# Gates, sums and layer norm between layers in one block, with the next weights' loads, and a last stage that stores by groups

## The chip, the cores and the metric

The kernel runs on 1 core of one Trainium2 chip. The metric is the device time of one execution in microseconds. The kernel before takes 5393.07 us, the median of 3 runs (5383.29 to 5398.34).

## The reference

The model has four layers on x of 16 sequences of 256 tokens of 128 features (4096 rows). Each layer normalises x, computes an attention branch s and a feed-forward branch g from the normalised rows, and adds their gated product:

```python
for layer in range(4):
    xn = _layernorm(x)              # (x - mean) / sqrt(var + 1e-5) over the 128 features
    s = attention[layer](xn)        # linear, gelu linear, causal softmax, small heads
    g = silu(feed_forward[layer](xn))   # local transformer, experts, routed, grouped
    x = x + s * g
return x
```

The last feed-forward is grouped: rows are cut into 8 groups of 512, and for each group h1 = x W1^T + b1 (128 to 512), h2 = h1 W2^T + b2 (512 to 128).

## The kernel before, in words

All rows stay in the core's memory: `core.x`, `core.xn` (normalised), `core.s` (attention branch), `core.y` (feed-forward branch) are each 128 partitions by 32 tiles by 128 features, `core.xnt` is the transpose of `xn` (features on partitions). One tile is 128 rows.

The program is a list of stages, one after the other (`stages`, lines 2969 to 2987). Each stage opens semaphores with `signals`, which clears them and puts a barrier of all engines; then comes a block, in which each engine has its own program and waits on semaphores; the block ends with a meeting of all engines, and `zero()` clears the semaphores again, with a barrier. So no engine starts on a stage before all engines have ended the one before.

For one layer the stages are these four.

- `layer_norm_stage` (line 297): VectorE takes the statistics of all 32 tiles (`bn_stats`, line 280), aggregates them (line 289), then computes 1/sqrt of the 32 variances in a chain of small operations, each waiting for the one before (lines 291 and 221 to 227), and writes the normalised rows, one scalar operation for each tile with mean and root as columns (line 293). TensorE transposes each tile (line 321), ScalarE copies four transposes at a time (line 329).
- the attention stage. Those of layers 0 and 1 begin by loading their weights with `load` (line 253), a block of its own that ends when all have landed; then comes the block that computes.
- the feed-forward stage. That of layer 0 uses the memory of `core.x` as room for other things, and so leaves in `core.x_in_memory` where the first x lies in DRAM.
- `combine_stage` (line 370): in four groups of 8 tiles ScalarE applies Silu to `core.y` (line 388), VectorE multiplies by `core.s` (line 394) and adds to `core.x` (line 398). In layer 0 SyncE issues the four loads of x there (line 383).

`grouped_ffn_stage` (from line 2834) is the last feed-forward. SyncE issues four loads for each of the 8 groups in its block (lines 2855 to 2858). TensorE turns W2 of group n (line 2867), multiplies W1 and b1 of group n - 1 by it (lines 2875 and 2878), and applies the merged matrix to the rows of group n - 2 (line 2888); ScalarE copies the turned W2 (line 2905), VectorE keeps the merged matrix and writes the group's 4 tiles to `core.y` (line 2920). After it `combine_stage` runs over all rows, and then one DMA stores all of x (line 2946).

`load(core, [x, ident])` at the start of the program (line 2938) loads all of x in one DMA, with the identity, in a block of its own.

Of the kernel before, what the change touches and what calls it, by code (L numbers as in the profile page):

```python
# [14 lines left out]
F32 = mybir.dt.float32  # L15
I32 = mybir.dt.int32
BF16 = mybir.dt.bfloat16
ALU = mybir.AluOpType
# [3 lines left out]
P = 128  # L22
# [124 lines left out]
def chain(eng, sem):  # L147

    n = [0]

    def after(ins):
        n[0] += 1
        ins.then_inc(sem, 1)
        eng.wait_ge(sem, n[0])

    return after
# [73 lines left out]
class Core:  # L230


    def __init__(self, nc, dram, ctx):
        self.nc, self.dram, self.stage, self.x_in_memory = nc, dram, 0, None
# [62 lines left out]
def layer_norm_stage(core):  # L297

    nc, bank, G = core.nc, core.bank, 4
    with ExitStack() as ctx:  # L300
        stats = ctx.enter_context(nc.sbuf_tensor(core.name("ln_stats"), [P, NT, 6], F32))
        mv = ctx.enter_context(nc.sbuf_tensor(core.name("ln_mv"), [P, NT, 2], F32))
        rstd = ctx.enter_context(nc.sbuf_tensor(core.name("ln_rstd"), [P, NT], F32))
        tmp = ctx.enter_context(nc.sbuf_tensor(core.name("ln_tmp"), [P, NT], F32))
        (dve_step, rows_ready, turned, copied), zero = ctx.enter_context(
            signals(nc, [core.name(n) for n in ("ln_dve_step", "ln_rows_ready", "ln_turned", "ln_copied")]))
        with nc.Block() as block:
            @block.vector
            def _(dve):
                after = chain(dve, dve_step)  # L310
                tiles = [core.x[:, j, :] for j in range(NT)]
                for ins in normalise_rows(nc, after, tiles, [core.xn[:, j, :] for j in range(NT)], stats, mv, rstd, tmp, 1e-5):
                    ins.then_inc(rows_ready, 1)

            @block.tensor
            def _(pe):
                for j in range(NT):
                    pe.wait_ge(rows_ready, j + 1)
                    if j % G == 0 and j >= 2 * G:
                        pe.wait_ge(copied, j // G - 1)  # L320
                    ins = nc.tensor.transpose(bank[j // G % 2][:, (j % G) * P:(j % G + 1) * P], core.xn[:, j, :], core.ident[:, :])
                    if j % G == G - 1:
                        ins.then_inc(turned, 1)

            @block.scalar
            def _(act):
                for g in range(NT // G):
                    act.wait_ge(turned, g + 1)
                    nc.scalar.copy(core.xnt[:, g * G * P:(g + 1) * G * P], bank[g % 2][:, :]).then_inc(copied, 1)
        zero()  # L330
# [39 lines left out]
def combine_stage(core):  # L370

    nc, G = core.nc, 8
    reload, core.x_in_memory = core.x_in_memory, None
    with ExitStack() as ctx:
        (gated, multiplied, added), zero = ctx.enter_context(signals(nc, [core.name(n) for n in ("cb_gated", "cb_multiplied", "cb_added")]))
        x_in, zero_in = ctx.enter_context(signals(nc, [core.name(f"cb_x_in{i}") for i in range(NT // G)]))
        groups = [slice(i * G, (i + 1) * G) for i in range(NT // G)]
        with nc.Block() as block:
            @block.sync
            def _(sp):  # L380
                if reload is not None:
                    for i, g in enumerate(groups):
                        sp.dma_start(core.x[:, g, :], reload[:, g, :]).then_inc(x_in[i], 16)

            @block.scalar
            def _(act):
                for g in groups:
# [2602 lines left out]
```

## Time and profile before

| what | value |
|---|---|
| median of 3 runs | 5393.07 us |
| profiled execution | 5392.81 us, of which 5391.0 us are the span of the trace |
| busy, share of the span | TensorE 88%, weight loads 62%, VectorE 69%, ScalarE 52%, GpSimd 52% |
| mean granted TensorE clock | 0.934 |

Busy time is an average over stages that are very unlike each other: the feed-forward stage of layer 0 alone (in which TensorE is nearly always busy) fills the first 3570 us or so. The stages run one after the other, so a passage between two stages is to be read by itself, in the timeline.

### The profile page before, as it was taken

To read this page: it belongs to the slowest core of one execution; us is meant where nothing else is said; L and a number is where in the kernel's file an instruction comes from. 1 tells how busy PE (TensorE), PEld (TensorE's weight loads), DVE (VectorE), ACT (ScalarE), POOL (GpSimd) and SP (SyncE) were. 2 spreads that over 40 slices of the span, in tenths; PEclk is the share of its full clock that TensorE was granted. 3 is DMA by queue.
4 is the path that set the end of the run, shared out by engine and by line. 5 is a ranking of instruction groups with operands and counts; after the bars stand their busy time and mean duration, and the time that the engine had idled before them with its cause. 6 is when DMAs were issued, how large, how long until landed. Compare 5 with 4: busy or idle time off the path is not lost. (4 is left out here: it accounts for less than half of the span.)

```text
span 5391.0 us, 143191 instructions
## 1 busy us (share of the span) xinstructions
PE 4720.6 (88%) x57069; PEld 3338.6 (62%) x57103; DVE 3708.4 (69%) x8589; ACT 2807.9 (52%) x6208; POOL 2810.1 (52%) x3349
## 2 busy tenths in 40 slices
PE   7699999999999999999999999955375999845886
PEld 3367676666667767666676667744363667623665
DVE  7677777777777777777777777746725656577443
ACT  2266666666666666666666666621023666641342
POOL 4477776777677767776777777701122333311000
PEclk9799999999999999999999999977587999967898
DMA  0211111111111111111111110000211000010012
GB/s 21 66 35 25 25 35 37 25 25 33 32 29 25 35 31 29 25 35 33 29 25 34 22 28 21 18 24 2 77 52 24 2 2 2 1 25 13 26 29 58
DMA packets 312165, 150.62 MB, mean 28 GB/s; under 512 B 146143, under 2 KB 301004, under 8 KB 311244
## 3 DMA queue, kind: packets, MB, share of 16 engines
q1 hardware_dynamic: 309451, 137.20, 10.5%
q8 instruction: 461, 7.55, 0.6%
q0 software_dynamic: 2048, 4.20, 0.3%
q14 instruction: 205, 1.67, 0.1%
HBM read 101.10 MB, written 27.41 MB: 24 GB/s over the span
## 5 line engine op out<-in xcount | busy, mean ns | idle before, releaser
L1450 POOL TENSOR_TENSOR loc_a<-loc_a,loc_b 128x512 f32<-128x512 f32 x768 | 977.2, 1272 | 598.3 <-DVE loc_b L1526 598.3
L1127 PE MATMUL psum<-loc_wqk,loc_xt 128*128 128x512 f32 x1536 | 837.6, 628 | 12.3 <-DVE loc_b L1526 5.9
L1195 PE MATMUL psum<-loc_m,xn_rows 128*128 128x128 f32 x6144 | 843.7, 280 | 3.8 <-DVE y_rows L1558 2.6
L1475 POOL TENSOR_TENSOR loc_a<-loc_a,loc_rn 128x512 f32<-128x512 f32 x768 | 784.9, 1043 | 0.1
L1195 PEld LDWEIGHTS psum<-loc_m,xn_rows 128*128 128x128 f32 x6144 | 745.6, 192 | 55.9 <-issue 36.0
L1319 ACT ACTIVATE loc_sq<-psum 128x512 f32<-128x512 f32 x768 | 456.1, 594 | 449.6 <-PE psum L1127 443.2
L1522 DVE TENSOR_TENSOR loc_a<-psum,loc_rope 128x512 f32<-128x512 f32 x768 | 523.9, 682 | 174.9 <-ACT loc_sq L1319 161.7
L1356 ACT COPY xn_rows<-psum 128x512 f32<-128x512 f32 x768 | 412.3, 589 | 326.6 <-PE psum L1183 324.3
L1482 POOL TENSOR_TENSOR xn_cols<-xn_cols,loc_rec 128x512 f32<-128x512 f32 x384 | 392.3, 1042 | 307.5 <-DVE loc_rec L1553 307.5
L1135 PEld LDWEIGHTS psum<-ident,loc_a 128*128 128x128 f32 x3072 | 347.7, 142 | 317.9 <-issue 307.1
L1526 DVE TENSOR_TENSOR loc_b<-psum,loc_rope 128x512 f32<-128x512 f32 x768 | 520.8, 678 | 0.0
L1530 DVE TENSOR_REDUCE loc_n<-loc_sq 128x8 f32<-128x512 f32 x768 | 517.1, 673 | 0.0
L1135 PE MATMUL psum<-ident,loc_a 128*128 128x128 f32 x3072 | 477.0, 278 | 10.4 <-ACT loc_qt L1337 7.2
L769 POOL TENSOR_TENSOR l2a_p<-l2a_p,l2a_rec 128x256 f32<-128x256 f32 (+1 forms) x256 | 211.5, 826 | 441.5 <-DVE l2a_rec L756 441.5
L1183 PE MATMUL psum<-xn_cols,loc_x 64*128 64x256 f32 x3072 | 435.6, 402 | 1.1 <-ACT xn_rows L1356 0.9
L1537 DVE TENSOR_REDUCE loc_top<-psum 128x8 f32<-128x512 f32 x384 | 247.3, 686 | 236.7 <-PE psum L1158 236.7
L1337 ACT COPY loc_kt<-psum 128x512 f32<-128x512 f32 x384 | 224.7, 585 | 306.2 <-PE psum L1135 306.2
L1158 PE MATMUL psum<-loc_kt,loc_qt 64*32 64x64 f32 x24576 | 333.8, 223 | 3.2 <-issue 2.5
L1158 PEld LDWEIGHTS psum<-loc_kt,loc_qt 64*32 64x32 f32 x24576 | 295.0, 105 | 50.8 <-issue 39.6
L1168 PEld LDWEIGHTS psum<-ident,xn_cols 128*128 128x128 f32 x1536 | 181.2, 141 | 225.1 <-issue 225.1
L1127 PEld LDWEIGHTS psum<-loc_wqk,loc_xt 128*128 128x128 f32 x1536 | 232.7, 191 | 122.2 <-issue 59.7
L1183 PEld LDWEIGHTS psum<-xn_cols,loc_x 64*128 64x128 f32 x3072 | 264.4, 186 | 67.2 <-issue 10.4
(370 smaller groups left out, 8532.2 us busy)
## 6 DMA issues: line engine op xcount, KB each, us to landing
loc_x<-loc_shifted SPq DMA_DIRECT2D x192, 256.0 KB, 4.0
loc_shifted<-y_rows SPq DMA_DIRECT2D x144, 64.0 KB
loc_wqk<-in_L_ffn_Wqkv SPq DMA_DIRECT2D x24, 256.0 KB, 3.8
x_rows<-y_rows SPq DMA_DIRECT2D x96, 64.0 KB
x_rows<-y_rows SPq DMA_DIRECT2D x96, 63.5 KB
moe_w<-in_L_ffn_W SPq DMA_DIRECT2D x16, 256.0 KB, 5.0
l3a_qk<-l3a_rot SPq DMA_DIRECT2D x16, 256.0 KB, 2.1
grp_w<-in_L_ffn_W SPq DMA_DIRECT2D x16, 256.0 KB, 4.2
```

The costliest lines, as they stand in the source:

```text
L1127: nc.tensor.matmul(ring("p", i, unit), xt[:, b % 2, t * P:(t + 1) * P], wqk[:, unit * 512:(unit + 1) * 512], start=True, stop=True).then_i ...
L1135: last = nc.tensor.transpose(turn_bank[:, j * P:(j + 1) * P], a[:, (UNITS * i + unit) % (3 * UNITS), j * P:(j + 1) * P], core.ident[:, :])
L1158: last = nc.tensor.matmul(score_bank[h][32 * w:32 * w + 32, 64 * j:64 * j + 64], qt[rows_h, i % 2, j, 32 * w:32 * w + 32], kt[rows_h, b % ...
L1183: last = nc.tensor.matmul(u_bank[h][:, 256 * v:256 * v + 256], x2[rows_h, b % 3, WPT * t + w, :], pt[rows_h, i % 2, :, 32 * w:32 * w + 32] ...
L1195: last = nc.tensor.matmul(y_bank[:, 0:P], u[:, i % 2, h // 2, h % 2, :], m[:, h, :], start=(h == 0), stop=(h == HEADS - 1))
L1319: nc.scalar.activation(sq[:, g % 2, :], ring("p", i, unit), ACT.Square).then_inc(sem["squared"], 1)
L1356: nc.scalar.copy(to, u_bank[h].rearrange("p (w j q) -> p w j q", w=2, j=PAIRS)).then_inc(sem["u_copied"], 1)
L1450: nc.gpsimd.tensor_tensor(part, part, b_[:, g % 2, :], ALU.add).then_inc(sem["added"], 1)
L1475: nc.gpsimd.tensor_tensor(part, part, rn[:, i % 2, 8 * unit:8 * unit + 8].rearrange("p (h e) -> p h e", e=1).to_broadcast([P, 8, DH]), ALU ...
L1522: nc.vector.tensor_tensor(a[:, g % (3 * UNITS), :].rearrange("p (h d) -> p h d", d=DH), src.rearrange("p (h d) -> p h d", d=DH), cos, ALU. ...
L1526: nc.vector.tensor_tensor(b_[:, g % 2, :].rearrange("p (h s d) -> p h s d", s=2, d=32), halves, sin, ALU.mult).then_inc(sem["rotated"], 1)
L1530: nc.vector.tensor_reduce(n2[:, i % 2, 8 * unit:8 * unit + 8], sq[:, g % 2, :].rearrange("p (h d) -> p h d", d=DH), AX.X, ALU.add).then_in ...
```

## The change

- `combine_stage` of a layer and `layer_norm_stage` of the next are one block, `enter_layer_stage`. Silu stays with ScalarE in four groups of 8 tiles. The products go to GpSimd. VectorE adds group by group and takes the statistics of each group right after its sum. Aggregation and the chain of the root are done for each half of the tiles (16 each): for the first half after two groups, for the second at the end. GpSimd normalises the 16 tiles of the first half, VectorE those of the second. TensorE and ScalarE transpose and copy as before.
- The weights of the attention of layers 0 and 1, and of the grouped feed-forward (biases of all 8 groups, matrices of the first four), are loaded by SyncE in that block; it waits for them at its end. The loading blocks of those stages go. The other attention stages keep their loads.
- At the start of the program x comes in four DMAs by the same block (layer 0, without gates, products and sums), and the identity and the weights behind it.
- `grouped_ffn_stage` loads the matrices of groups 4 to 7 itself, applies Silu (ScalarE), product (GpSimd) and sum (VectorE) to each group of 4 tiles after its store, and stores each group of x to DRAM in a DMA of its own. The last `combine_stage` and the single store go.

```diff
-def combine_stage(core):
-def layer_norm_stage(core):
...
+def enter_layer_stage(core, weights=None):
+    nc, bank, layer = core.nc, core.bank, core.layer
+    core.layer += 1
+    G, T, HALF = 8, 4, NT // 2
+    arriving, core.x_in_memory = core.x_in_memory, None
+    core.weights = weights(core) if weights else None
+    loads = core.weights.loads if weights else []
...
+            @block.sync
+            def _(sp):
+                if arriving is not None:
+                    for i, g in enumerate(groups):
+                        sp.dma_start(core.x[:, g, :], arriving[:, g, :]).then_inc(sem[f"x_in{i}"], 16)
+                if layer == 0:
+                    sp.dma_start(core.ident[:, :], core.dram["ident"]).then_inc(sem["ident_in"], 16)
+                for dst, src in loads:
+                    sp.dma_start(dst, src).then_inc(sem["loaded"], 16)
+                if loads:
+                    sp.wait_ge(sem["loaded"], 16 * len(loads))
+
+            @block.vector
+            def _(dve):
+                after = chain(dve, sem["dve_step"])
+
+                def gather(i, g):
+                    if arriving is not None:
+                        dve.wait_ge(sem[f"x_in{i}"], 16)
+                    if layer > 0:
+                        dve.wait_ge(sem["multiplied"], i + 1)
+                        nc.vector.tensor_tensor(core.x[:, g, :], core.y[:, g, :], core.x[:, g, :], ALU.add).then_inc(sem["added"], 1)
+                        dve.wait_ge(sem["added"], i + 1)
+                    for j in range(g.start, g.stop):
+                        last = nc.vector.bn_stats(stats[:, j, :], core.x[:, j, :])
+                    return last
+
+                def measure(h):
+                    for j in range(h.start, h.stop):
+                        last = nc.vector.bn_aggr(mv[:, j, :], stats[:, j, :])
+                    after(last)
+                    after(nc.vector.tensor_scalar(mv[:, h, 1], mv[:, h, 1], 1e-5, None, ALU.add))
+                    rsqrt(nc, after, rstd[:, h], mv[:, h, 1], tmp[:, h])
+
+                for n, h in enumerate(halves):
+                    for i in (2 * n, 2 * n + 1):
+                        last = gather(i, groups[i])
+                    after(last)
+                    measure(h)
+                    scales.append(after.count[0])
+                for j in range(HALF, NT):
+                    nc.vector.tensor_scalar(core.xn[:, j, :], core.x[:, j, :], mv[:, j, 0:1], rstd[:, j:j + 1], ALU.subtract,
+                                            ALU.mult).then_inc(sem["dve_rows"], 1)
+
+            @block.gpsimd
+            def _(pool):
+                if layer > 0:
+                    for i, g in enumerate(groups):
+                        pool.wait_ge(sem["gated"], i + 1)
+                        nc.gpsimd.tensor_tensor(core.y[:, g, :], core.y[:, g, :], core.s[:, g, :], ALU.mult).then_inc(sem["multiplied"], 1)
+                pool.wait_ge(sem["dve_step"], scales[0])
+                for j in range(HALF):
+                    nc.gpsimd.tensor_scalar(core.xn[:, j, :], core.x[:, j, :], mv[:, j, 0:1], rstd[:, j:j + 1], ALU.subtract,
+                                            ALU.mult).then_inc(sem["pool_rows"], 1)
...
 def grouped_ffn_stage(core):
...
             @block.sync
             def _(sp):
+                for g in range(NG // 2, NG):
+                    for dst, src in own.matrices(core, g, w1[g], w2[g]):
+                        sp.dma_start(dst, src).then_inc(late[g - NG // 2], 16)
                 for g in range(NG):
-                    sp.dma_start(w2[:, g, :, :], dram["L3_ffn_W2"][g, :, :].rearrange("p (c o) -> p c o", o=P)).then_inc(loaded[g], 16)
...
+                    sp.wait_ge(sem["added"], g + 1)
+                    sp.dma_start(core.out[:, rows(g), :], core.x[:, rows(g), :]).then_inc(sem["sent"], 16)
+                sp.wait_ge(sem["sent"], 16 * NG)
...
             @block.scalar
...
+                for n in range(NG + 3):
+                    if n < NG:
+                        keep_turned(n)
+                    if 0 <= n - 3 < NG:
+                        gate(n - 3)
...
             @block.vector
...
-                for n in range(NG + 2):
+                for n in range(NG + 4):
                     if 0 <= n - 1 < NG:
                         keep_merged(n - 1)
                     if 0 <= n - 2 < NG:
                         store(n - 2)
+                    if 0 <= n - 4 < NG:
+                        add(n - 4)
...
 def stages():
     return [
+        lambda core: enter_layer_stage(core, LinearWeights), linear_attention_stage, local_transformer_stage,
+        lambda core: enter_layer_stage(core, GeluWeights), gelu_linear_attention_stage, experts_stage,
+        enter_layer_stage, causal_attention_stage, routed_ffn_stage,
+        lambda core: enter_layer_stage(core, GroupedWeights), small_head_attention_stage, grouped_ffn_stage,
     ]
```

## Rows read from the trace of the kernel before

**Rows 1.** Page, part 1: busy us of each engine, share of the span, instructions.

```profile
PE 4720.6 (88%) x57069; PEld 3338.6 (62%) x57103; DVE 3708.4 (69%) x8589; ACT 2807.9 (52%) x6208; POOL 2810.1 (52%) x3349
```

**Rows 2.** Timeline, layer 0 to 1: start, duration in us, engine, line, idle before, releaser.

```profile
3573.03 1.28 ACT L388 ACT_TABLE_LOAD   x1 [7.21 <-PEq L141]
3573.05 4.06 SPq L383 DMA_DIRECT2D x_rows<-in_L_attn_x  x4
3575.42 1.23 DVE L394 TENSOR_TENSOR y_rows<-y_rows,s_rows 128x1024 f32<-128x1024 f32 x1 [6.03 <-ACT y_rows L388]
3577.50 1.23 DVE L398 TENSOR_TENSOR x_rows<-y_rows,x_rows 128x1024 f32<-128x1024 f32 x1 [0.85 <-DMA x_rows<-in_L_attn_x]
...
3587.50 6.28 DVE L280 BATCH_NORM_STATS2 ln_stats<-x_rows 128x6 f32<-128x128 f32 x32 [1.60 <-PEq L141]
3593.82 2.22 DVE L289 BATCH_NORM_AGGREGATE ln_mv<-ln_stats 128x2 f32<-128x6 f32 x32
...
3598.97 8.29 DVE L293 TENSOR_SCALAR xn_rows<-x_rows,ln_mv,ln_rstd 128x128 f32<-128x128 f32 x32
...
3607.69 0.58 ACT L329 COPY xn_cols<-psum 128x512 f32<-128x512 f32 x1 [0.44 <-PE psum L321]
...
3619.54 0.87 PE L1663 MATMUL psum<-ident,l1a_w 128*128 128x128 f32 x3 [11.89 <-PEq L141]
```

**Rows 3.** Timeline, layer 1 to 2.

```profile
4064.13 1.28 ACT L388 ACT_TABLE_LOAD   x1 [33.68 <-PEq L141]
...
4097.79 0.58 ACT L329 COPY xn_cols<-psum 128x512 f32<-128x512 f32 x1 [0.44 <-PE psum L321]
```

**Rows 4.** Timeline, the start of the program.

```profile
1.54 0.91 SPq L261 DMA_DIRECT2D x_rows<-in_L_attn_x  x1
...
13.18 6.28 DVE L280 BATCH_NORM_STATS2 ln_stats<-x_rows 128x6 f32<-128x128 f32 x32 [13.18 <-PEq L141]
...
33.37 0.58 ACT L329 COPY xn_cols<-psum 128x512 f32<-128x512 f32 x1 [0.44 <-PE psum L321]
...
43.43 1.65 PE L435 MATMUL psum<-l0a_w,xn_cols 128*128 128x384 f32 x2 [10.11 <-DVE l0a_ones L549]
```

**Rows 5.** Timeline, the last feed-forward stage.

```profile
5330.65 0.37 SPq L2855 DMA_DIRECT2D grp_w<-in_L_ffn_W  x1
...
5337.77 1.11 PE L2867 MATMUL psum<-ident,grp_w 128*128 128x128 f32 x4 [9.95 <-DMA grp_b<-in_L_ffn_b]
...
5339.81 1.11 PE L2867 MATMUL psum<-ident,grp_w 128*128 128x128 f32 x4 [0.92 <-DMA grp_b<-in_L_ffn_b]
...
5365.99 0.69 DVE L2920 TENSOR_TENSOR y_rows<-psum,grp_offset 128x512 f32<-128x512 f32 x1 [0.20 <-PE psum L2888]
```

**Rows 6.** GpSimd's groups by shape: busy us, mean ns of one, idle before.

```profile
L1450 POOL TENSOR_TENSOR loc_a<-loc_a,loc_b 128x512 f32<-128x512 f32 x768 | 977.2, 1272 | 598.3 <-DVE loc_b L1526 598.3
...
L364 POOL TENSOR_TENSOR s_rows<-s_rows,l1a_gamma 128x1024 f32<-128x1024 f32 x2 | 4.9, 2447 | 16.3 <-DVE s_rows L293 16.3
...
L2373 POOL TENSOR_SCALAR cd_w1h<-cd_w1h,cd_gh 128x512 f32<-128x512 f32 x1 | 1.6, 1633 | 0.0
L2372 POOL TENSOR_SCALAR cd_w1l<-cd_w1l,cd_gl 128x64 f32<-128x64 f32 x1 | 0.5, 477 | 0.0
```

**Rows 7.** Timeline, VectorE's operations while GpSimd works and while it doesn't.

```profile
4765.32 8.27 POOL L2369 TENSOR_TENSOR y_rows<-xn_rows,cd_rn 128x512 f32<-128x512 f32 x8
...
4770.57 0.98 DVE L2436 SCALAR_TENSOR_TENSOR cd_base<-cd_base,cd_top 16x1 f32<-16x1 f32 x1
...
4773.66 0.14 DVE L2436 SCALAR_TENSOR_TENSOR cd_base<-cd_base,cd_top 16x1 f32<-16x1 f32 x1
...
3712.63 16.80 DVE L293 TENSOR_SCALAR s_rows<-s_rows,bn_mv,bn_rstd 128x128 f32<-128x128 f32 x32
```

**Rows 8.** Page, part 6: DMAs of 256 KB, us from issue to landing.

```profile
l3a_qk<-l3a_rot SPq DMA_DIRECT2D x16, 256.0 KB, 2.1
grp_w<-in_L_ffn_W SPq DMA_DIRECT2D x16, 256.0 KB, 4.2
```

More of the change, by code:

```diff
@@ L325, in _ @@
             @block.scalar
             def _(act):
-                for g in range(NT // G):
-                    act.wait_ge(turned, g + 1)
-                    nc.scalar.copy(core.xnt[:, g * G * P:(g + 1) * G * P], bank[g % 2][:, :]).then_inc(copied, 1)
+                if layer > 0:
+                    for g in groups:
+                        nc.scalar.activation(core.y[:, g, :], core.y[:, g, :], ACT.Silu).then_inc(sem["gated"], 1)
+                for q in range(NT // T):
+                    act.wait_ge(sem["turned"], q + 1)
+                    nc.scalar.copy(core.xnt[:, q * T * P:(q + 1) * T * P], bank[q % 2][:, :]).then_inc(sem["copied"], 1)
@@ L367, in layer_norm_of_branch @@
         zero()
-def combine_stage(core):
[L372 to L387, printed above, removed]
-                    nc.scalar.activation(core.y[:, g, :], core.y[:, g, :], ACT.Silu).then_inc(gated, 1)
-            @block.vector
-            def _(dve):
-                for i, g in enumerate(groups):
-                    dve.wait_ge(gated, i + 1)
-                    nc.vector.tensor_tensor(core.y[:, g, :], core.y[:, g, :], core.s[:, g, :], ALU.mult).then_inc(multiplied, 1)
-                    dve.wait_ge(multiplied, i + 1)
-                    if reload is not None:
-                        dve.wait_ge(x_in[i], 16)
-                    nc.vector.tensor_tensor(core.x[:, g, :], core.y[:, g, :], core.x[:, g, :], ALU.add).then_inc(added, 1)
-        zero()
-        zero_in()
 def linear_attention_stage(core):
@@ L559, in linear_attention_stage @@
         zero()
+    own.ctx.close()
 class Softmax:
@@ L1802, in gelu_linear_attention_stage @@
         layer_norm_of_branch(core, 1e-12, gamma[:, :], beta[:, :])
+    own.ctx.close()
 def experts_stage(core):
@@ L2905, in _, with gate @@
                     nc.scalar.copy(w2t[:, g % 2, :, :], turn_bank[g % 2].rearrange("p (c q) -> p c q", c=CH)).then_inc(sem["w_ready"], 1)
+                def gate(g):
+                    act.wait_ge(sem["stored"], g + 1)
+                    nc.scalar.activation(core.y[:, rows(g), :], core.y[:, rows(g), :], ACT.Silu).then_inc(sem["gated"], 1)
+                for n in range(NG + 3):
[3 more added lines that the diff above has]
+                        gate(n - 3)
+            @block.gpsimd
+            def _(pool):
+                for g in range(NG):
+                    pool.wait_ge(sem["gated"], g + 1)
+                    nc.gpsimd.tensor_tensor(core.y[:, rows(g), :], core.y[:, rows(g), :], core.s[:, rows(g), :], ALU.mult).then_inc(sem["multiplied"], 1)
             @block.vector
```

164 lines of the change are left out of this document (89 added, 75 removed).

## The prediction

> **What bounds the kernel now.** I read first the page's busy times: TensorE is busy 4720.6 us, 88% [rows 1], but nearly all of that lies inside the long stages, which the change leaves alone. Then I read the timeline at the four places where one layer hands over to the next, and at the end. There nearly every engine idles while one works. Between layers 0 and 1 [rows 2]: from the table load for the Silu (3573.03) to the end of the last copy (3607.69 + 0.58 = 3608.27) are 35.24 us, and VectorE works in 30 of them: products and sums (3575.42 to 3585.90, where the wait of 1.60 begins), statistics (6.28), aggregation (2.22), the root's chain of 13 small operations (3593.82 + 2.22 = 3596.04 to 3598.97, 2.93 us) and 32 rows of 0.26 us (8.29). Then nothing runs for 11.27 us until the weights, whose loads start only now, let TensorE begin (3619.54). The place after layer 1 is the same without the wait for x (0.85 in rows 2): 34.24 us [rows 3]; the one after layer 2 is its like, so there are two of these, and their next stages load for themselves, which doesn't change. At the start [rows 4], VectorE waits for all of x until 13.18, the last copy ends at 33.95, the first product of the attention is at 43.43: 9.48 us of loading. At the end [rows 5], TensorE waits for the first weights from 5330.65 to 5337.77, the last group is stored at 5366.68, and the remaining 24.3 us are Silu, products, sums and one store of all of x one after the other.
>
> **Barriers.** Between the last sum and the statistics VectorE waits 1.60 us [rows 2]; three clearings with their barriers and the block's ends lie there, so one barrier is about 0.5 us, and 1.5 us is what stays of a passage without loads.
>
> **Start of the program.** x comes in quarters. The reload's first quarter, issued at 3573.05, let the sum start at 3577.50 [rows 2], some 4.3 us later; from 1.54 [rows 4] that is 5.9. Eight statistics are 6.28 / 4 = 1.6. The second quarter is in at about 7.8 (2 MB had landed by about 11.5, as VectorE starts at 13.18 after barriers); its statistics end at 9.4, 16 aggregations 1.1 and the chain 2.9 give 13.4. From there GpSimd normalises the first 16 tiles.
>
> **The price of a GpSimd row** is the term that decides, and no row has it: a 128x128 scalar operation with two scalars of a column each. With one such scalar 128x64 took 477 ns and 128x512 took 1633 [rows 6]; on the line between them 128 elements are 0.64 us. The lower bound is the line of the two-input operations, 2447 ns at 1024 and 1272 at 512 [rows 6], so 0.39 at 128; the upper is twice 0.64 = 1.28, if the second operation is a second pass. I take 0.75 (0.64 and a little for the second scalar), with its handover 0.8. VectorE's price for the same row is 0.26 [rows 2].
>
> **Who blocks whom.** GpSimd ran eight operations in a row from 4765.32, 8.27 us [rows 7]. Inside it VectorE's operation on one element with two inputs took 0.98 us, right behind it, without GpSimd, 0.14. And 32 rows of the kind that take 8.29 us alone took 16.80 us from 3712.63, with GpSimd's products over part of it. So VectorE's sums, two-input chain operations and rows wait for the end of the GpSimd operation in progress; GpSimd waits as long for them. The statistics read one tensor and I cost them free. During a row of GpSimd operations VectorE then gets one such operation through for each.
> The Trainium skill (SBUF — State Buffer, Who interferes with whom) has this as a rule: GpSimd and VectorE share one port pair, taken for a whole instruction, and VectorE needs it in two-port modes or with two inputs from SBUF against a GpSimd operation that reads. By that rule the new block's parallel work is largely serial again, and the sum is the one below; without it the sum would be the first rival's.
>
> Start, continued: VectorE does the other statistics (3.1, to 16.6) and aggregation (17.7), four chain operations on one input (0.9, 18.6), nine on two inputs at 0.8 each (25.8). GpSimd ends at 13.4 + 16 x 0.8 = 26.3. The 16 rows left take 4.15 (30.4), transposing and copying the last group 1.0 as in rows 2 (3607.26 to 3608.27): 31.3, against 33.95: **-2.6**. The nine weights are issued behind x and land long before. So the 9.48 us of loading become a passage of 1.5: **-8.0**. Together -10.6.
>
> **Between the layers**, clock from the table load. Silu of group 0 is done at 2.4 (3573.03 to 3575.42). GpSimd multiplies 2.45 us a group [rows 6] where VectorE took 1.2: 2.4 to 4.85, and goes straight on with group 1 (to 7.3), so the first sum waits for that. Sum 1.2 (8.5), product 2 (to 10.95) beside the statistics, sum 1 (12.15), product 3 (14.6) beside statistics (13.8) and aggregation (14.9), chain 2.9: 17.8. Now GpSimd's 16 rows of 0.8 plus the two sums that hold it up for 1.2 each: 17.8 + 12.8 + 2.4 = 33.0. VectorE: sum 2 waits one row (18.6 to 19.8), statistics (21.4), sum 3 (21.8 to 23.0), statistics (24.6), aggregation (25.7), four chain operations (26.6), eight at 0.8 until GpSimd is through, one more (33.2), 16 rows (37.4), tail 1.0: 38.4. Before: 34.2. One barrier pair of the old combining block goes (0.5). So **+3.7** each after layers 1 and 2; after layer 0 38.4 - 35.24 - 0.5 = +2.7 (x is in at 4.4, before the first product is), and the 11.27 of loading become 1.5: **-7.1** in all.
> Cover of the loads: SP's queue. Layer 3's 24 loads (eight matrices, sixteen vectors) are the most; before, eight loads of these kinds were in 9.16 us after the first issue (5330.65 to 5339.81, rows 5), so 24 at that pace are 27.5 us, under 38. If they weren't, the block's end would wait for them. In layer 1 eleven loads queue behind x's four quarters, nothing that VectorE waits for stands behind them.
>
> **The last stage.** The block starts as before at about 5330.6, but groups 0 to 3 are there: 7.1 us off, and 0.9 for the wait of group 1 [rows 5]. Groups 4 to 7 are issued at once and land about 4.2 us after issue [rows 8], needed over 12 us later. TensorE's cadence stays, as the added Silu and sum stand behind the copies and stores that TensorE waits for, on engines with slack. Tail from the last store at 5366.68 (old clock): Silu of half a width 0.6; GpSimd is then still at group 6's product (1.27 us, to 67.7), group 7's to 69.0, sums of 0.7 for 6 and 7 to 70.4. The 256 KB store: 2.1 to 4.2 us for that size [rows 8], I take 3.1; two clearings that the old end didn't have 1.0, close 0.4: 75.0. Against 5391.0 that is -16.0, and with the 8.1 at the start **-24.1**.
>
> **Sum.** -10.6 - 7.1 + 2 x 3.7 - 24.1 = -34.4 us. The profiled execution took 5392.8 (span 5391.0 and 1.8 around it), the median of the runs is 5393.1: 5358.4, so 5358.
>
> **Bounds.** With a row at 0.39 on GpSimd (0.45 with handover): GpSimd ends at 27.4, the chain at 29.0, rows and tail 34.2, so -0.5 twice, -11.3 after layer 0, -15.0 at the start: -51 in all, 5341. With 1.28 (1.33): 17.8 + 21.3 + 2.4 = 41.5, end 46.2, so +11.5 twice, +0.7, -2.8 at the start: -3, 5390. That is about 60 us per us of a row.
>
> **Rivals.**
> A, nothing blocks: on other shapes or forms of operands the two engines may run beside each other, as VectorE's statistics do. Then the chain ends at 14.5, GpSimd's rows at 26.5, TensorE's 16 last transposes (0.26 each) and a copy at 31.3: -3.4 twice, -14.2, -11.6 at the start, -24.1: 5335. For it: GpSimd's own times hardly vary. Against it: rows 7.
> B, GpSimd's rows become the bound at 1.05 to 1.6 us: the gain of loads and end is given back in three blocks, within 16 us (0.3%, what this measurement can tell from none): about 5385. For it: its scalar form is dearer per element (1633 at 512) than the two-input one (1272).
> C, slower: the same place at 2.0 us a row, beyond twice the one-scalar price. Each us costs 64 here (16 rows, four blocks), so from the -3 at 1.28: +43, 5436; it is slower than can be overlooked from 1.6 us on. Against it: no row of that kind.
> D, the prefetch doesn't help, because the loads outlast their block: for layer 3 they would have to take over 38 us, 1.6 each; it would cost a few us only: within the range.
>
> **Chances.** Forecast (row 0.55 to 1.05, blocking): 0.60, own range 5346 to 5377. A, or a still cheaper row: 0.22. B: 0.12. C: 0.05; D 0.01. Faster 0.83, same 0.12, slower 0.05. Range: 5334 to 5384, from A's time into B's.
>
> **What would show it.** In the new block: GpSimd's row between 0.6 and 0.9 us; a sum of VectorE of 2 to 3.5 us instead of 1.22, or started late, while a product runs; chain operations of 0.8 instead of 0.19 in the second half; VectorE's rows ending 37 us after the table load. Passages without loads of 1.5 us; first transposes of the last stage 2.5 us after the previous copy; the last store issued 4 us after the last group. Wrong: sums of 1.22 us beside products (A), rows over 1 us (B, C), or a block that ends on SP's wait (D).

## The result and the profile after

The changed kernel takes 5344.54 us, the median of 4 runs (5338.56 to 5351.56), beside 5392.26 us before (4 runs, 5383.29 to 5398.34): ratio 0.9913, 95% interval 0.9894 to 0.9932. Measured again on another chip it took 5342.65 us (5 runs) beside 5389.07 (9 runs), ratio 0.9913 (0.9895 to 0.9931). Forecast were 5358, range 5334 to 5384: the time lies in the range, but 1.5 us below the 5346 to 5377 that the prediction gave its own case, and the gain is 47.7 us where 34.4 were forecast.

The profiled execution took 5351.56 us, the slowest of its four, with a span of 5349.7, against 5392.8 and 5391.0. The page's busy times move little (TensorE's by +23 us), but for GpSimd's, which grow by 103 us beside [rows 1]:

```profile
span 5349.7 us, 142952 instructions
PE 4743.6 (89%) x57103; PEld 3342.8 (62%) x57103; DVE 3698.6 (69%) x8565; ACT 2811.1 (53%) x6212; POOL 2913.3 (54%) x3433
```

So the gain is in the passages, and they must be read one by one. The start of the program, from the timeline (start, duration, engine, line, operation, idle before, releaser), beside [rows 4]:

```profile
5.63 1.64 DVE L404 BATCH_NORM_STATS2 en_stats<-x_rows 128x6 f32<-128x128 f32 x8 [5.63 <-DMA x_rows<-in_L_attn_x]
...
13.11 12.73 POOL L432 TENSOR_SCALAR xn_rows<-x_rows,en_mv,en_rstd 128x128 f32<-128x128 f32 x16 [12.66 <-DVE en_rstd L228]
...
21.21 4.46 DVE L421 TENSOR_SCALAR xn_rows<-x_rows,en_mv,en_rstd 128x128 f32<-128x128 f32 x16
...
25.89 4.18 PE L446 MATMUL psum<-ident,xn_rows 128*128 128x128 f32 x17 [0.34 <-POOL xn_rows L432]
...
30.11 0.59 ACT L457 COPY xn_cols<-psum 128x512 f32<-128x512 f32 x1 [0.41 <-PE psum L446]
...
32.05 1.65 PE L527 MATMUL psum<-l0w_w,xn_cols 128*128 128x384 f32 x2 [1.99 <-DVE l0a_ones L641]
```

The first product comes at 32.05 instead of 43.43. GpSimd's 16 rows take 12.73 us, 0.80 each. All 64 of its rows, by their tile (shortest, median and longest in ns, first and last start in us):

```profile
L432 POOL TENSOR_SCALAR xn_rows<-x_rows,en_mv,en_rstd x64: 783/797/1828, 13.1 to 4912.3; 128x128 f32<-128x128 f32 x64
```

The block between layers 1 and 2, beside [rows 3] (that between layers 0 and 1 [rows 2] is like it, 36.25 us long):

```profile
4038.13 1.28 ACT L454 ACT_TABLE_LOAD   x1 [33.64 <-PEq L141]
...
4040.56 11.23 POOL L429 TENSOR_TENSOR y_rows<-y_rows,s_rows 128x1024 f32<-128x1024 f32 x4 [10.30 <-ACT y_rows L454]
4042.95 3.35 DVE L401 TENSOR_TENSOR x_rows<-y_rows,x_rows 128x1024 f32<-128x1024 f32 x1 [10.27 <-POOL y_rows L429]
...
4055.22 1.23 DVE L401 TENSOR_TENSOR x_rows<-y_rows,x_rows 128x1024 f32<-128x1024 f32 x1
4055.30 14.24 POOL L432 TENSOR_SCALAR xn_rows<-x_rows,en_mv,en_rstd 128x128 f32<-128x128 f32 x16 [3.50 <-DVE en_rstd L228]
...
4062.53 0.32 DVE L222 TENSOR_SCALAR en_tmp<-en_mv 128x16 int32<-128x16 int32 x1
...
4064.45 0.17 DVE L226 TENSOR_TENSOR en_tmp<-en_rstd 128x16 f32<-128x16 f32 x1
4064.65 0.17 DVE L227 TENSOR_TENSOR en_tmp<-en_tmp,en_mv 128x16 f32<-128x16 f32 x1
...
4064.86 0.33 DVE L228 SCALAR_TENSOR_TENSOR en_rstd<-en_tmp,en_rstd 128x16 f32<-128x16 f32 x1
...
4066.00 4.54 DVE L421 TENSOR_SCALAR xn_rows<-x_rows,en_mv,en_rstd 128x128 f32<-128x128 f32 x16
...
4069.59 3.90 PE L446 MATMUL psum<-ident,xn_rows 128*128 128x128 f32 x17 [0.35 <-POOL xn_rows L432]
...
4072.81 1.30 ACT L457 COPY xn_cols<-psum 128x512 f32<-128x512 f32 x2 [0.27 <-PE psum L446]
```

The first sum takes 3.35 us where it takes 1.22 alone: it waits until GpSimd's second product is through. VectorE's rows are done at 4070.54, only a microsecond behind GpSimd's (4069.54). What ends the block is TensorE: it transposes the tiles in order, waits until 4069.5 for GpSimd's last, and makes that one and VectorE's 16 in a row from there (x17). ScalarE's copies of them end at 4074.11, 35.98 us after the table load.

The end, beside [rows 5]:

```profile
5310.67 0.37 ACT L2838 COPY s_rows<-psum 128x256 f32<-128x256 f32 x1 [0.80 <-PE psum L2775]
...
5313.45 1.94 PE L2961 MATMUL psum<-ident,l3w_w 128*128 128x128 f32 x8 [2.82 <-PEq L141]
...
5341.05 0.68 DVE L3035 TENSOR_TENSOR x_rows<-y_rows,x_rows 128x512 f32<-128x512 f32 x1
...
5341.65 0.68 DVE L3030 TENSOR_TENSOR y_rows<-psum,grp_offset 128x512 f32<-128x512 f32 x1
...
5342.25 3.71 DVE L3035 TENSOR_TENSOR x_rows<-y_rows,x_rows 128x512 f32<-128x512 f32 x3
```

TensorE starts 2.4 us after the previous stage's last copy instead of 9.5; the last group is written at 5342.33, and 7.4 us later all is over, where 24.3 followed before.

By places (microseconds; a second profile of the same kernel in the fourth column):

| place | before | after | after, again | forecast of the difference |
| --- | --- | --- | --- | --- |
| start to first product | 43.43 | 32.05 | 32.0 | -10.6 |
| table load to TensorE, layer 0 to 1 | 46.51 | 37.61 | 37.7 | -7.1 |
| the same, layer 1 to 2 | 48.3 | 50.2 | 50.6 | +3.7 |
| the same, layer 2 to 3 | 43.9 | 44.7 | 44.8 | +3.7 |
| last copy of the small heads to the end | 62.8 | 38.7 | 38.9 | -24.1 |
| sum of these | 244.9 | 203.3 | 204.0 | -34.4 |
| small-head attention, layer 3 | 377.4 | 384.6 | 373.9 | 0 |
| all the rest | 4768.7 | 4761.8 | 4762.9 | 0 |

### The profile page after: what moved, and what is told of

Read it like the earlier page. It is cut to its first block and busy times, and to the rows that moved or that the text cites. A ratio compares the mean times of both kernels' runs of the same rounds, so it can differ in the third digit from the quotient of the medians.

```text
span 5349.7 us, 142952 instructions
## 1 busy us (share of the span) xinstructions
PE 4743.6 (89%) x57103; PEld 3342.8 (62%) x57103; DVE 3698.6 (69%) x8565; ACT 2811.1 (53%) x6212; POOL 2913.3 (54%) x3433
## 5 line engine op out<-in xcount | busy, mean ns | idle before, releaser
L1288 PEld LDWEIGHTS psum<-loc_m,xn_rows 128*128 128x128 f32 x6144 | 744.9, 191 | 55.6 <-issue 35.4
L1276 PEld LDWEIGHTS psum<-xn_cols,loc_x 64*128 64x128 f32 x3072 | 264.4, 186 | 67.3 <-issue 10.7
```

The costliest lines, as they stand in the source:

```text
L1276: last = nc.tensor.matmul(u_bank[h][:, 256 * v:256 * v + 256], x2[rows_h, b % 3, WPT * t + w, :], pt[rows_h, i % 2, :, 32 * w:32 * w + 32] ...
L1288: last = nc.tensor.matmul(y_bank[:, 0:P], u[:, i % 2, h // 2, h % 2, :], m[:, h, :], start=(h == 0), stop=(h == HEADS - 1))
```

## The experiments

All start from the changed kernel. The first four were timed beside the kernel before at 5389.02 us (13 runs).

**Products on VectorE.**

```diff
...
                     if layer > 0:
+                        dve.wait_ge(sem["gated"], i + 1)
+                        nc.vector.tensor_tensor(core.y[:, g, :], core.y[:, g, :], core.s[:, g, :], ALU.mult).then_inc(sem["multiplied"], 1)
                         dve.wait_ge(sem["multiplied"], i + 1)
...
-                        nc.gpsimd.tensor_tensor(core.y[:, g, :], core.y[:, g, :], core.s[:, g, :], ALU.mult).then_inc(sem["multiplied"], 1)
```

> The products of the three blocks between layers go back from GpSimd to VectorE, nothing else changes. Theory (the sums wait for GpSimd's products, which take 2.45 us and hold the sums up, 3.3 and 1.7 us instead of 1.22): VectorE does product 1.2, sum 1.2 and statistics 1.65 of a group without waits, the first half's chain ends at 2.4 + 2 x 4.05 + 3.9 = 14.4 us after the table load instead of 17.1, GpSimd's rows at 27.2, the last copy at about 32 instead of 36.0: 4 us less in each of three blocks, -12 in all. Rival (GpSimd takes 4.9 us of products off VectorE, and the waits are only slack): the block gets longer by up to 4.9, +10 to +15 in all.

Measured: 5334.52 us (5328.81 to 5336.26), ratio 0.9898 (0.9881 to 0.9914). The blocks are 36.5, 34.5 and 35.0 us long instead of 36.3, 36.0 and 35.8: some 2 us in all, neither the gain nor the loss that was expected. The start of the rows shows where it went: they begin at 14.65 us instead of 17.17, but take longer:

```profile
4053.55 15.46 POOL L430 TENSOR_SCALAR xn_rows<-x_rows,en_mv,en_rstd 128x128 f32<-128x128 f32 x16 [22.47 <-DVE en_rstd L228]
```

15.46 us instead of 14.24, as two products more of VectorE stand in their way. What VectorE gains ahead of the rows it gives back in part beside them. After layer 0 it gains less ahead of them, as its first product comes only when x's first quarter is there, 4.2 us after the table load (3558.40) instead of 2.4:

```profile
3562.61 1.23 DVE L401 TENSOR_TENSOR y_rows<-y_rows,s_rows 128x1024 f32<-128x1024 f32 x1 [7.49 <-DMA x_rows<-in_L_attn_x]
```

The rest of the difference between the two profiles is the small-head stage, 368.3 us in this one (below).

**All rows on VectorE.**

```diff
-                for j in range(HALF, NT):
-                    nc.vector.tensor_scalar(core.xn[:, j, :], ...).then_inc(sem["dve_rows"], 1)
+                    for j in range(h.start, h.stop):
+                        nc.vector.tensor_scalar(core.xn[:, j, :], ...).then_inc(sem["dve_rows"], 1)
...
-                for j in range(HALF):
-                    nc.gpsimd.tensor_scalar(core.xn[:, j, :], ...).then_inc(sem["pool_rows"], 1)
```

> GpSimd normalises no rows: VectorE writes the 16 of each half right after that half's root. Products stay on GpSimd. Theory (16 rows are 12.7 to 14.2 us on GpSimd and 4.15 on VectorE, and the block ends when GpSimd's rows and then 16 transposes are through): between layers VectorE is through at 17.1 + 4.2 + 2 x 2.85 + 3.9 + 4.2 = 35.1, last copy 36.0, as now; at the start 13.0 + 4.2 + 3.2 + 3.9 + 4.2 = 28.5, last copy 29.4 instead of 30.7. In all -1, no difference that can be told. Rival (GpSimd's rows are a gain, as they run beside VectorE): +4.2 in each of four blocks, +17.

Measured: 5339.94 us (5338.00 to 5340.71), ratio 0.9909 (0.9892 to 0.9926). The blocks take 36.19, 36.20 and 36.19 us, within 0.4 of the changed kernel's; at the start the last copy ends at 29.7 instead of 30.7. GpSimd's 51 us of rows in four blocks buy nothing. Why: the same place, between layers 1 and 2:

```profile
4070.14 4.19 DVE L420 TENSOR_SCALAR xn_rows<-x_rows,en_mv,en_rstd 128x128 f32<-128x128 f32 x16
4070.55 4.32 PE L438 MATMUL psum<-ident,xn_rows 128*128 128x128 f32 x16 [9.44 <-DVE xn_rows L420]
```

Here VectorE's second half is the last work and transposes run beside it. In the changed kernel that work is done sooner, but the transposes come after it.

**Loads back where they were.** The loading blocks stand at the head of the attention stages of layers 0 and 1 again, and the last stage issues all its loads itself.

```diff
-    loads = core.weights.loads if weights else []
+    loads = []
...
+        load(core, own.loads)
...
-                for g in range(NG // 2, NG):
+                for g in range(NG):
```

> No weights are loaded in the blocks between layers: the attention of layers 0 and 1 load in a block of their own as before, the grouped feed-forward loads all in its own block. Theory (the loads are fully hidden in the new kernel): +8.0 at the start, +9.8 after layer 0, +7.1 in the last stage, +25 in all; the blocks between layers keep their lengths (30.7 and 36). The small-head attention took 384.6 us in the profile of the changed kernel against 377.5 before. If the weights that lie in memory during it or their loads are the cause, it is back at 377; if it is a variation between executions, it falls anywhere between, whatever is loaded. Rival (part of the prefetch is paid in the blocks): less than +20.

Measured: 5370.43 us (10 runs, 5356.22 to 5381.30), ratio 0.9959 (0.9948 to 0.9971), 26 more than the changed kernel. Places: first product at 40.2 (+8.2), between layers 0 and 1 46.9 us from table load to TensorE (+9.3), first product of the last stage 9.0 us after the copy (+6.6), together 24.1; the eight groups of the last stage take 0.8 us more besides (29.6 instead of 28.9), which makes the 25 expected:

```profile
3607.49 0.59 ACT L457 COPY xn_cols<-psum 128x512 f32<-128x512 f32 x1 [0.41 <-PE psum L446]
3609.68 0.34 SPq L263 DMA_DIRECT2D l1w_w<-in_L_attn_Wq  x1
...
3618.67 0.88 PE L1752 MATMUL psum<-ident,l1w_w 128*128 128x128 f32 x3 [11.22 <-PEq L141]
```

The blocks keep their length (36.35, 36.37 and 35.61 us; the first and the last of them have the loads beside them in the changed kernel, 36.25 and 35.79), so the loads cost nothing where they stand now. The small-head stage took 377.5 us, as in the kernel before. Alone that would fit its rival, that the weights in memory slow it; but it took 377.5 in the kernel with products of half a width too, which has the loads ahead, and the last two experiments take this up.

**The old end.** Its edit takes the stores, gates, products and sums out of the last block and runs the old stages behind it:

```diff
-                for g in range(NG):
-                    sp.wait_ge(sem["added"], g + 1)
-                    sp.dma_start(core.out[:, rows(g), :], core.x[:, rows(g), :]).then_inc(sem["sent"], 16)
...
+def combine_stage(core):
+    ...
+def store_stage(core):
+    ...
```

> The last stage only writes its branch, then come the old combining block over all rows and the single store; the weights of groups 0 to 3 are still loaded ahead. Theory (tail of 24.3 us from the last store of the branch to the end before, 7.4 now, and a cadence of 3.11 us a group that is TensorE's either way): +17. Rival (the added Silu, product, sum and DMA of each group slow the groups): the 8 groups become shorter than the present 28.9 us from first transpose to last store of the branch, and the difference is below +15.

Measured: 5368.56 us (5359.51 to 5375.46), ratio 0.9957 (0.9940 to 0.9973). From the last group's write to the end 24.91 us instead of 7.37, that is +17.5; the groups before it take 28.6 us against 28.9, so what was added between them costs 0.3 us (where, see the last stage below). The medians' 24 are more than that; the small-head stage, 388.0 us here, varies by as much.

**Products of half a width.** To see whether a sum waits for the GpSimd operation in progress or for the whole run of them.

```diff
-                        dve.wait_ge(sem["multiplied"], i + 1)
+                        dve.wait_ge(sem["multiplied"], 2 * (i + 1))
...
-                        nc.gpsimd.tensor_tensor(core.y[:, g, :], core.y[:, g, :], core.s[:, g, :], ALU.mult).then_inc(sem["multiplied"], 1)
+                        for part in (slice(g.start, g.start + 4), slice(g.start + 4, g.stop)):
+                            nc.gpsimd.tensor_tensor(core.y[:, part, :], core.y[:, part, :], core.s[:, part, :],
+                                                    ALU.mult).then_inc(sem["multiplied"], 1)
```

> GpSimd multiplies each group of 8 tiles in two operations of 4 tiles (1.2 to 1.3 us each) instead of one of 2.45. Theory (a sum of VectorE waits for the end of the GpSimd operation in progress, then runs at its own speed): the first sum of a block takes 1.2 + 1.2 = 2.4 us instead of 3.35. Rival (the two engines share the memory's bandwidth as long as both run): it stays near 3.3, as GpSimd's products fill the same time. The block's length changes by less than 1 us either way.

```profile
4041.21 11.79 POOL L430 TENSOR_TENSOR y_rows<-y_rows,s_rows 128x512 f32<-128x512 f32 x8 [10.30 <-ACT y_rows L456]
4043.73 2.27 DVE L401 TENSOR_TENSOR x_rows<-y_rows,x_rows 128x1024 f32<-128x1024 f32 x1 [10.41 <-POOL y_rows L430]
```

The first sum takes 2.27 us instead of 3.35: 1.1 us less, about half a product. So it waits for the operation in progress. One run took 5345.06 us; the blocks 35.98, 35.82 and 35.57.

**GpSimd's rows as operations on two inputs.** The same 16 rows, each as two operations that read x and the root's column. This kernel leaves out the mean of these tiles and serves for its times alone.

```diff
-                    nc.gpsimd.tensor_scalar(core.xn[:, j, :], core.x[:, j, :], mv[:, j, 0:1], rstd[:, j:j + 1], ALU.subtract,
-                                            ALU.mult).then_inc(sem["pool_rows"], 1)
+                    for part in (spare[:, j, :], core.xn[:, j, :]):
+                        ins = nc.gpsimd.tensor_tensor(part, core.x[:, j, :], rstd[:, j:j + 1].to_broadcast([P, P]), ALU.mult)
+                    ins.then_inc(sem["pool_rows"], 1)
```

> GpSimd writes each of its 16 rows with two operations of two inputs (x by the root, spread over the row; the first into a spare tile), about 0.35 us each, instead of one scalar operation of 0.8: it is busy about as long, with another kind of operation. Left out: the mean is not subtracted in these 16 tiles. Open is why VectorE's root chain took only 3.68 us (17.46 to 21.14 at the start of the program) beside GpSimd's scalar rows, where I had 8.1. Theory (a scalar operation on GpSimd reaches into memory only part of its time, an operation with two inputs nearly all of it): beside these rows VectorE's nine chain operations on two inputs take 0.3 to 0.5 us instead of 0.17 to 0.33, the chain 4.5 us or more, and its 16 rows in part too over 4.5 us. Rival (operations of 16 elements are too short to be held up much by anything): chain of 3.7 us or less as now.

```profile
4049.37 1.22 DVE L402 TENSOR_TENSOR x_rows<-y_rows,x_rows 128x1024 f32<-128x1024 f32 x1
4049.41 1.44 POOL L434 TENSOR_TENSOR en_spare<-x_rows,en_rstd 128x128 f32<-128x128 f32 x1 [3.48 <-DVE en_rstd L228]
...
4058.72 0.33 DVE L226 TENSOR_TENSOR en_tmp<-en_rstd 128x16 f32<-128x16 f32 x1
4058.97 0.39 POOL L434 TENSOR_TENSOR xn_rows<-x_rows,en_rstd 128x128 f32<-128x128 f32 x1
4059.08 0.32 DVE L227 TENSOR_TENSOR en_tmp<-en_tmp,en_mv 128x16 f32<-128x16 f32 x1
4059.33 0.39 POOL L434 TENSOR_TENSOR en_spare<-x_rows,en_rstd 128x128 f32<-128x128 f32 x1
```

Beside these every operation of the chain takes 0.32 us and they follow each other by 0.36, the distance of GpSimd's own: one passes for each of GpSimd's, as the prediction had it for all GpSimd work. Both ways: a GpSimd operation of 0.39 us that meets a sum takes 1.44. The 13 operations of the chain take 4.5 us, against 3.6 beside the scalar rows (4056.31 to 4060.83 here). One run took 5326.02 us; its blocks are 35.5, 35.5 and 35.4, and its small-head stage 368.1.

**The first half's rows on ScalarE**, with the products on VectorE, and then with the products on GpSimd. The core of both:

```diff
-                    nc.gpsimd.tensor_scalar(core.xn[:, j, :], ...)
...
+                        if j < HALF:
+                            nc.scalar.activation(core.xn[:, j, :], core.x[:, j, :], ACT.Identity, bias=minus[:, j:j + 1],
+                                                 scale=rstd[:, j:j + 1]).then_inc(sem["pool_rows"], 1)
```

`minus`, the mean times the root with its sign turned, is one more operation of VectorE.

> Products on VectorE, and ScalarE, which is idle after the Silu, writes the first half's 16 rows (root as scale, one more small operation on VectorE for the bias -mean x root); GpSimd does nothing in the block. Theory (what ends the block is GpSimd's 16 rows and the 16 transposes behind them; without them it is VectorE's own work): first half's chain at 14.6, VectorE's second half 8.1 + 3.9 to 26.7, 16 rows to 30.9, last copy at 31.8 after the table load instead of 36.0, at the start 26 instead of 30.7: -4.2 in three blocks and -4.7, -17 in all against the changed kernel. Rival (VectorE and the handovers bound the block either way): blocks of 34 to 35 as with the products alone, -5 in all.

> As the changed kernel, products on GpSimd, but the first half's 16 rows on ScalarE. Theory: first half's chain at 17.3 (the sums of the first half still wait for products, 2.7 us), then VectorE without neighbours: two sums and statistics 5.7, 3.9, 4.2, so 31.1 and last copy at 32.0; at the start 26 as with e7. -4 in three blocks and -4.7 against the changed kernel, -17: taking the products away from GpSimd brings nothing beyond. Rival (the products are the costlier part): blocks of 34 to 35.

Measured beside the kernel before at 5393.32 us (7 runs): 5327.00 us (5323.48 to 5333.28), ratio 0.9870 (0.9854 to 0.9887), with the products on VectorE; 5332.78 us (5326.86 to 5341.11), ratio 0.9888 (0.9872 to 0.9905), on GpSimd. The blocks: 34.2, 32.3, 32.2 and 32.2, 32.3, 32.2; the last copy of the start ends at 25.6 in both, where 30.7 was. In the first kernel VectorE's first product after layer 0 waits for x's reload, as above, hence 34.2. But for that block both theories hold (31.8 and 32.0 expected), and the rivals' 34 to 35 falls: once GpSimd has no rows, it makes no difference to the later blocks which of the two engines multiplies. The second kernel:

```profile
4049.71 3.19 ACT L459 ACTIVATE xn_rows<-x_rows,en_minus,en_rstd 128x128 f32<-128x128 f32 x8 [12.10 <-DVE en_minus L421]
4050.26 3.17 PE L446 MATMUL psum<-ident,xn_rows 128*128 128x128 f32 x8 [44.16 <-ACT xn_rows L459]
...
4059.39 4.19 DVE L425 TENSOR_SCALAR xn_rows<-x_rows,en_mv,en_rstd 128x128 f32<-128x128 f32 x16
4059.79 4.32 PE L446 MATMUL psum<-ident,xn_rows 128*128 128x128 f32 x16 [2.32 <-DVE xn_rows L425]
```

ScalarE's rows follow each other by 0.40 us, half of GpSimd's 0.80, and hinder VectorE in nothing that is seen: 16 rows 4.19, as where VectorE writes all of them, and the first half is transposed long before the second comes. VectorE's rows end 31.2 us after the table load, against 32.4 in the changed kernel. So of the 3.7 us by which this block is shorter, 1.3 are VectorE's earlier end, and 2.4 are the transposes that no longer stand behind GpSimd's rows.

**The changed kernel and the last one again**, on one chip.

> The changed kernel once more, nothing edited. Theory: the small-head stage of layer 3 takes between 368 and 388 us in one execution and another whatever the program (377.4 in the kernel before, 384.6 in the changed one, 368.1 to 388.0 in the experiments), while the blocks between the layers repeat within 0.4 us. So this profile shows blocks of 36.2 +- 0.4 us (from table load to the end of the last copy) after each layer, a start of 32.0, a tail of 7.4, and a small-head stage that differs from 384.6 by several us, with the span moved by the same; the median is 5344 +- 6. Rival: 384.6 us is a property of the changed kernel (its loads or its placement in memory slow that stage): then the stage is within 2 us of 384.6 again.

> The kernel of the experiment in which ScalarE normalises the first sixteen tiles, once more and beside the changed kernel on the same chip. Theory: its three blocks are 3.8 us shorter each and its start 5 us shorter, 16.4 in all, so the difference of the medians is 16 us once the varying stage is averaged over more runs (11.7 were measured with four runs of each). Rival: it is less than 8 us, because TensorE's stages behind the shorter blocks take back what the blocks gain.

Measured beside 5389.07 us (9 runs): 5342.65 us (5339.29 to 5351.89), and 5328.78 us (5326.84 to 5332.61), ratio 0.9887 (0.9867 to 0.9906). The small-head stage in four profiles, as stretches (from, to, length; busy us of TensorE, its weight loads, VectorE, ScalarE, GpSimd; granted clock; DMA share; GB/s): after, after again, the kernel with two-input rows, the old end.

```profile
4926.40:5311.00 384.60, 332.80 (x5312) 237.18 (x5312) 157.36 (x304) 136.16 (x289) 20.35 (x16) 0.87 0.08 24
```

```profile
4928.00:5301.90 373.90, 327.21 (x5312) 233.16 (x5312) 157.50 (x304) 136.04 (x289) 20.33 (x16) 0.88 0.08 25
```

```profile
4917.40:5285.50 368.10, 320.39 (x5312) 229.66 (x5312) 157.45 (x304) 135.88 (x289) 20.29 (x16) 0.90 0.08 26
```

```profile
4929.90:5317.90 388.00, 337.23 (x5312) 240.88 (x5312) 157.52 (x304) 136.43 (x289) 20.34 (x16) 0.86 0.08 24
```

The same number of instructions, the same kernel even in the first two, and 10.7 us apart; in these four, the longer the stage, the lower its granted clock (0.86 to 0.90) and the longer TensorE is busy. The rival, that 384.6 belongs to the changed kernel, falls. Where two profiles have this stage alike, 373.9 and 373.8, their spans are 5340.8 and 5324.7: ScalarE's rows are worth 16.1 us, where 16.4 were expected and the blocks and starts of these two profiles give 16.9; the medians say 13.9, and the rival's less than 8 falls. Which of the two kernels with ScalarE's rows is faster is not shown: the medians were 5327.00 with the products on VectorE and 5332.78 on GpSimd, with ranges that overlap, while the blocks of the second are 2 us shorter in all.

## Why the prediction held, and where not

The time fell into the stated range, and the loads, the price of a row and the last stage came as reckoned; what happens inside the blocks between layers did not.

**Start, forecast -10.6, came -11.4.** GpSimd's rows began at 13.1 (13.4 forecast), took 0.80 each with handover (0.80) and ended at 25.8 (26.3). Passage to the first product 1.4 us (1.5). The mechanism at the end was another: not VectorE's rows, but the transposes behind GpSimd's.

**The price of a row**, which decided, was right: 0.797 us in the median, inside the bounds of 0.39 and 1.28, and the value taken was 0.75.

**A sum beside products**: forecast 3.7 for the wait and the sum (4.85 to 8.5), came 3.35. The half-width products show that the wait ends with the operation in progress. The chain of the first half ends at 17.1 (17.8 forecast). The third sum was to wait for a row of GpSimd; it was issued first instead, took 1.23 us, and GpSimd's first row took the 1.83 above.

**The step that failed: "eight at 0.8 until GpSimd is through".** It took the 0.98 us of one operation beside GpSimd's two-input products [rows 7] for the price of every two-input operation beside any GpSimd work. Beside the scalar rows the chain of 13 operations took 3.6 us between the layers (25.7 to 33.2, 7.5 us, forecast) and 3.7 at the start (8.1 forecast); undisturbed it is 2.7. Only one in three of the nine on two inputs waits, for 0.15 us, and three of them pass in 0.78 us, the time of one row. In the changed kernel the one that waits is always line 228's; it is the moment that counts and not the form, for in the kernel with the loads back it is line 226's at the start of the program:

```profile
20.15 0.32 DVE L226 TENSOR_TENSOR en_tmp<-en_rstd 128x16 f32<-128x16 f32 x1
```

The two-input rows of the experiment bring back one operation for each of GpSimd's. Two things that were costed free of any hold weren't: of the four chain operations on one input three took 0.32 to 0.39 us instead of 0.17 (all four 1.35 us, 0.9 forecast), and VectorE's 16 rows take 4.5 us beside GpSimd's, where 4.15 were forecast.

The trace of the kernel before could have told this. The prediction reads the 0.14 us of 4773.66 [rows 7] as an operation without GpSimd beside it. But GpSimd was at work then, on one of the very scalar operations of [rows 6], and the same operation took 0.14 inside the next one too:

```profile
4773.58 0.48 POOL L2372 TENSOR_SCALAR cd_w1l<-cd_w1l,cd_gl 128x64 f32<-128x64 f32 x1
4773.66 0.14 DVE L2436 SCALAR_TENSOR_TENSOR cd_base<-cd_base,cd_top 16x1 f32<-16x1 f32 x1
...
4774.05 1.63 POOL L2373 TENSOR_SCALAR cd_w1h<-cd_w1h,cd_gh 128x512 f32<-128x512 f32 x1
...
4775.08 0.14 DVE L2436 SCALAR_TENSOR_TENSOR cd_base<-cd_base,cd_top 16x1 f32<-16x1 f32 x1
```

So the 0.98 and the 0.14 differ by the form of GpSimd's operation, and not by whether GpSimd works.

The Trainium skill (SBUF — State Buffer, Who interferes with whom) says that whoever issues first has the shared pair for its whole instruction. For GpSimd's two-input operations the runs agree (3.35 and 2.27 us for the sum, 0.32 for each of the chain). For its scalar operation they don't: two-input operations of 0.17 us passed inside a row of 0.78. The measurement decides; for this form the runs show VectorE held up in a part of the instruction alone. Why, no run here tells.

**What took its place.** VectorE's rows end 32.4 us after the table load; with the last group's transposes and copy (1.0) the block would end at 33.4. It ends at 36.0, as TensorE has VectorE's 16 tiles still to transpose, 0.23 us each, and may not begin them before GpSimd's last: it takes them in order. This is the end that the prediction wrote down for rival A, with the first half as it wrote it down for the forecast: 31.4 + 4.6 = 36.0 instead of 33.0 + 4.4 + 1.0 = 38.4. So the two places after layers 1 and 2 cost 2.7 us together where 7.4 were forecast, and the one after layer 0 gained 8.9 instead of 7.1. Together these are 6.5 of the 7.2 us by which the places' sum (-41.6) exceeds the forecast. (The blocks alone cost 3.2, 34.24 to 35.98 and 34.34 to 35.79. Of the 0.5 us taken off for a barrier pair the passage behind the block shows nothing after layer 1, 14.1 and 14.3 us, and 0.7 after layer 2, 9.6 and 8.9.) No run gives TensorE the tiles in another order, or GpSimd some of them but fewer.

**Loads.** Forecast were -8.0 at the start and -9.8 between layers 0 and 1; the passages left are 1.4 us each (9.48 and 11.27 before), so -8.1 and -9.9, and taken back the loads cost 8.2 and 9.3. Layer 3's 24 loads are all issued 12.5 us after the table load of their block and held up nothing: rival D is out.

**Last stage, forecast -24.1, came -24.1**, by terms of -7.1, nothing and -17.0 instead of -7.1, -0.9 and -16.0: that the sum agrees is luck. The wait of 0.92 us is gone, but the clock granted to TensorE is 0.50 (1.2 GHz) in these first groups in either kernel, whether it had been idle for 10.0 us ahead of them (before) or for 2.8 (after), and 1.00 (2.4 GHz) from about the third group on. Stretches of before, then of after:

```profile
5340.70:5342.40 1.70, 1.70 (x10) 1.70 (x9) 0.00 (x0) 0.58 (x1) 0.00 (x0) 0.50 0.80 261
5342.40:5343.50 1.10, 1.10 (x10) 1.10 (x9) 0.00 (x0) 0.00 (x0) 0.00 (x0) 0.80 1.09 226
5343.50:5346.60 3.10, 3.10 (x30) 3.10 (x29) 0.98 (x4) 0.58 (x1) 0.00 (x0) 1.00 0.97 270
```

```profile
5317.10:5319.00 1.90, 1.90 (x11) 1.90 (x11) 0.00 (x0) 0.00 (x0) 0.00 (x0) 0.52 1.10 368
5319.00:5322.00 3.00, 3.00 (x30) 3.00 (x29) 0.97 (x4) 0.59 (x1) 0.00 (x0) 1.00 0.87 280
```

So part of what was waiting is slow work now: 0.4 us of the 0.9 were left at the third group's transposes (5.3 us after the first operation instead of 5.7). Not even they are seen at the last group, whose write ends 28.9 us after the first operation in both kernels. There the prediction's step that the cadence stays is off by 0.3: the sum of an earlier group (5341.05, 0.68 us) now stands on VectorE between its last two writes, which start 1.21 us apart instead of 0.89, and 0.90 with the old end, which has no sum there. The tail is 1.0 us shorter than forecast: the last sum was over 3.6 us after the last group's write (3.7 forecast), and store and close took 3.7 where 3.1 + 1.0 + 0.4 were put down.

**The rest of the 47.7 us.** The places give 41.6. The medians' interval, 0.9895 to 0.9931 of 5389, is 37 to 57 us and holds that. No change is known to act on the long stages, in which the profiles differ by -6.9 and -5.8 us besides the small heads, and those alone vary by 20. With one profile of the kernel before it stays open whether these 6 us are more than that.

**Rivals.** A (nothing blocks, 5335; its own terms add up to 5336) was nearer in time, 9.5 us from the 5344.5 where the forecast's 5358 is 13.5 off, and wrong in its reason: sums are held up, and the whole block is not 31 but 36 us. The mechanism lies between the two as well: two-input operations of GpSimd hold VectorE up, its scalar ones little. B and C are out with the row's price. The range held because A's time was its lower end.

## What to carry to other kernels

Before work is split between two engines, look at who consumes it, and in what order: a half that is finished early by the faster engine gains nothing while the in-order consumer still waits for the other half, and then the consumer's whole second half lies bare. Here ScalarE's 0.40 us rows, beside which VectorE's operations kept their times, gained 16 us where GpSimd's 0.80 us rows gained none. (Whether another order of the tiles would have saved GpSimd's half was not tried.) When one row of a trace is to give the price of work beside another engine, look up what that engine was doing at that moment, and with which form of operation. And when a small change is judged by medians, find the stage that varies by itself and compare profiles in which it is alike.

## What the hardware showed that was not expected

GpSimd's scalar operation with two column operands (0.80 us for 128x128) lets two of three of VectorE's small two-input operations pass at 0.17 us; beside its two-input operation (0.39 us) each of them takes 0.32, one for each of GpSimd's. The hold goes both ways: a sum of 1.23 us stretched the row beside it from 0.80 to 1.83. ScalarE's rows of the same shape follow each other by 0.40 us, and while eight of them ran VectorE's sum took 1.23 us, as alone. One stage of equal instructions took from 368.1 to 388.0 us in eleven profiles of the changed kernel and its variants, with a granted clock from 0.90 down to 0.86; whether the clock is cause or effect no run here tells.
